# Five projections of an attention kernel moved within its four-step rhythm

## What is computed

```python
# layers 0, 1, 2, each with its own weights (W.T in layer 2)
q = heads(x @ W_q); k = heads(ctx @ W_k); v = heads(ctx @ W_v)
x = merge(softmax(q @ k.T / sqrt(8)) @ v) @ W_out + b_out + x

# layer 3: text = ctx[:, :73], ip = ctx[:, 73:]
probs_t = softmax(q @ k_t.T / sqrt(8))
text_out = merge(probs_t @ v_t)
qsem = l2norm(probs_t @ text)                  # per head, 256 channels
sem = qsem @ l2norm(ip).T
probs_ip = softmax(q @ k_ip.T / sqrt(8) + 0.5 * sem) * spatial_mask
x = (text_out + merge(probs_ip @ v_ip)) @ W_out + b_out + x
```

## Time and profile before

| what | us |
|---|---|
| median of 3 runs | 2264.24 |
| lowest, highest | 2257.44, 3683.89 |
| the profiled execution, its own time | 2264.95 |
| its span, first to last instruction | 2263.2 |
| PE busy with matmuls, weight loads | 2086.4, 1697.5 |
| DVE busy | 1481.7 |
| ACT busy | 1075.1 |
| POOL busy | 458.7 |

### The profile page before, as it was taken

How to read it: one execution, slowest core, us unless ns; L and a number is a source line. 1 busy time by engine, 2 the same in 40 slices (tenths; PEclk the granted TensorE clock), 3 DMA queues, 4 the chain that set the end, 5 groups by cost and what they waited for, 6 DMA issues and landing times.

```text
span 2263.2 us, 75842 instructions
## 1 busy us (share of the span) xinstructions
PE 2086.4 (92%) x26394; PEld 1697.5 (75%) x26394; DVE 1481.7 (65%) x4449; ACT 1075.1 (48%) x2733; POOL 458.7 (20%) x870
## 2 busy tenths in 40 slices
PE   2699999999999999999999999999999999999975
PEld 1567877887787788778778877887887788778764
DVE  3236776777677676767767766776676677667654
ACT  0245554455445455544545554554554455555431
POOL 0112122212212221221222122122212222222110
PEclk9889999999999999999999999999999999999975
DMA  3111111211111121112111111211211121111000
GB/s 82 49 43 50 52 43 42 52 50 39 47 52 44 41 52 51 38 46 52 45 41 52 52 38 47 53 44 40 52 52 38 47 53 44 39 53 38 22 10 5
DMA packets 108576, 101.31 MB, mean 45 GB/s; under 512 B 42240, under 2 KB 84952, under 8 KB 108184
## 3 DMA queue, kind: packets, MB, share of 16 engines
q1 hardware_dynamic: 104556, 92.88, 15.1%
q10 hardware_dynamic: 3628, 3.33, 0.6%
HBM read 34.13 MB, written 5.41 MB: 17 GB/s over the span
## 4 chain that ended last, share of the span: by engine, by line
PE 78%; SPq 8%; DVE 5%; issue 4%; DMA 2%; ACT 2%; ACTq 1%; DVEq 0%; POOLq 0%; POOL 0%
PE ps_s L738 11%; PE ps_c L816 10%; PE ps_s L771 8%; PE ps_c L886 6%; PE ps_k L839 6%; PE ps_k L644 5%; PE ps_q L717 5%; PE ps_c L875 4%; PE ps_k L670 4%; PE ps_s L788 4%; PE ps_k L844 4%; SPq L584 3%; PE ps_c L891 3%; PE ps_c L852 2%; SPq L577 2%
## 5 line engine op out<-in xcount | busy, mean ns | idle before, releaser
L1131 DVE TENSOR_REDUCE top<-ps_s 128x6 f32<-128x462 f32 (+3 forms) x1024 | 511.3, 546 | 88.2 <-PE ps_s L738 84.3
L1027 ACT ACTIVATE p_t<-ps_s 116x512 f32<-116x512 f32 (+1 forms) x768 | 372.9, 545 | 48.9 <-PE ps_s L771 46.9
L738 PE MATMUL ps_s<-k_blocks,q_sb 32*128 32x231 f32 (+1 forms) x3584 | 347.8, 384 | 20.3 <-issue 18.5
L816 PE MATMUL ps_c<-p_t,v_rows 116*27 116x128 f32 (+1 forms) x7168 | 288.7, 284 | 14.8 <-DMA v_rows<-v_img 12.3
L738 PEld LDWEIGHTS ps_s<-k_blocks,q_sb 32*128 32x128 f32 x3584 | 229.9, 185 | 84.9 <-issue 31.3
L816 PEld LDWEIGHTS ps_c<-p_t,v_rows 116*27 116x27 f32 (+1 forms) x7168 | 214.1, 108 | 86.5 <-issue 49.3
L1055 ACT ACTIVATE o_t<-ps_c 128x256 f32<-128x256 f32 x256 | 98.1, 383 | 368.3 <-PE ps_c L875 302.7
L1354 POOL TENSOR_TENSOR k_blocks<-k_sb,mask_k 128x231 f32<-128x231 f32 x384 | 211.8, 573 | 267.6 <-PE ps_s L771 252.5
L771 PE MATMUL ps_s<-q_sb,k_blocks 32*116 32x128 f32 (+1 forms) x5376 | 223.8, 283 | 27.7 <-DMA q_sb<-top_t 15.0
L839 PE MATMUL ps_k<-gram,p_t 116*128 116x154 f32 x896 | 210.6, 317 | 41.6 <-DVE weighted L1171 41.6
L771 PEld LDWEIGHTS ps_s<-q_sb,k_blocks 32*116 32x116 f32 (+1 forms) x5376 | 186.3, 175 | 63.7 <-issue 52.0
(11 more groups left out here) (118 smaller groups left out, 3595.3 us busy)
## 6 DMA issues: line engine op xcount, KB each, us to landing
v_rows<-v_img SPq DMA_DIRECT2D x128, 227.4 KB
context<-in_ctx SPq DMA_DIRECT2D x64, 336.0 KB, 3.0
q_sb<-top_t SPq DMA_DIRECT2D x576, 6.0 KB
v_rows<-v_img SPq DMA_DIRECT2D x64, 115.2 KB
v_rows<-v_img SPq DMA_DIRECT2D x64, 112.2 KB
v_rep<-v_dram SPq DMA_DIRECT2D x64, 50.0 KB
q_sb<-top_t SPq DMA_DIRECT2D x192, 2.0 KB
gram<-g_img SPq DMA_DIRECT2D x64, 46.3 KB
```

Of the source, the lines that this page charges most:

```text
L738: ins = pe.matmul(ps_s[:, z * 512 + j * GT:z * 512 + j * GT + n], q_sb[c % 3][lo:lo + QUAD, j * S:(j + 1) * S], k_blocks[c % 3][lo:lo + QU ...
L816: ins = pe.matmul(ps_c[t % 2][32 * (g % 4):32 * (g % 4) + UC, g // 4 * S:(g // 4 + 1) * S], v_rows[b % NC][0:n, v:v + UC], p_t[c % 3][0:n, ...
L1027: act.activation(to, source, ACT.Exp, scale=SCALE).then_inc(p_ready, 1)
L1131: dve.tensor_reduce(top[c % 2][:, z * BH:z * BH + m], s.rearrange("p (h t) -> p h t", t=T)[:, :, 0:n], AX.X, ALU.max).then_inc(s_top, 1)
```

## The change

It moves work between places of the four steps, and cuts the values in another way. No arithmetic is left out or added.

- `keys` of layers 1 and 2 go from step 2 to step 3, behind `queries` (PE); ACT copies them behind its `queries`.
- The waves go in the order z = 3, 0, 1, 2 (`BANKS`): the small one in step 1 behind `project_out`, z = 0 at that step's end, z = 1 in step 2 behind `project_out` (where the keys stood), z = 2 at its end.
- The values are made in two units, each with all three head slots of two layers: 224 and 112 columns (`values_unit`). The first stands in step 3 behind `project_out`, the second at the step's end, behind the Gram matrix, which itself moves behind `turn_back`. ACT copies each unit with three operations of 112 columns (`values_out`) instead of two of 224 and one of 224.
- ACT: in step 3 keys, products and values stand ahead of `text_exps`; the fourth of these goes to the step's end. `image_exp` of step 1 goes from between the exponents to behind `queries`.
- DVE: in step 0 steps 8 to 13 of the image branch go ahead of `results`, and 14 to 18 behind. In step 1 steps 19, 20 and the weights stand ahead of the weighing. In step 2 `results` goes ahead of `new_x`.

The core of the diff, first the step of the keys, the values and the waves:

```diff
-    if t % 8 == 2:
-        return 1, (t - 2) // 8
-    if t % 8 == 6:
-        return 2, (t - 6) // 8
+    if t % 8 == 3:
+        return 1, (t - 3) // 8
+    if t % 8 == 7:
+        return 2, (t - 7) // 8
...
+            def values_unit(b, u):
+                w = wv[:, :].rearrange("p (l k a n) -> p l k a n", l=L, k=2, a=2)[:, 2 * u:2 * u + 2]
+                third = w.rearrange("p l k a (g i d) -> p l k a g i d", g=TRI, i=2)
+                for kt in range(2):
+                    pe.matmul(ps_k[0:T, 0:2 * VN].rearrange("p (l n) -> p l n", l=2), cx(b, kt, 0, T),
+                              w[:, :, 0, kt, :], start=kt == 0, stop=kt == 1)
+                for kt in range(2):
+                    ins = pe.matmul(ps_k[0:T, 2 * VN:VU].rearrange("p (l g d) -> p l g d", l=2, g=TRI),
+                                    cx(b, kt, 0, T), third[:, :, 1, kt, :, 1, :], start=kt == 0, stop=kt == 1)
+                return ins
...
             def gram_wave(k, t, i):
-                z = 2 * (t % 4 - 1) + i
+                z = BANKS[2 * (t % 4 - 1) + i]
```

PE's function `step`:

```diff
-                if e_values(t):
-                    values(k, t)
+                if e_keys(t) and t % 4 == 3:
+                    keys(k, t)
                 if exists(t - 2):
                     product(k, t - 2)
                 if out(t):
                     project_out(k, t)
...
-                if e_gram(t):
-                    image(k, t)
-                if e_waves(t) and t % 4 == 1:
+                if e_values(t):
+                    values(k, t)
+                if e_waves(t):
                     gram_wave(k, t, 0)
-                if e_keys(t) and t % 4 == 2:
-                    keys(k, t)
...
                 if exists(t - 1):
                     second(k, t - 1)
-                if e_waves(t) and t % 4 == 2:
-                    gram_wave(k, t, 0)
                 if exists(t - 2):
                     turn_back(k, t - 2)
                 if e_waves(t):
                     gram_wave(k, t, 1)
                 if e_keys(t) and t % 4 == 0:
                     keys(k, t)
+                if e_gram(t):
+                    image(k, t)
                 if e_values(t):
                     values_rest(k, t)
```

ACT's:

```diff
+                if ip(t - 6):
+                    image_exp(k, t - 6)
+                if e_keys(t) and t % 4 == 3:
+                    keys(k, t)
+                if exists(t - 2):
+                    products(k, t - 2)
                 if e_values(t):
                     values(k, t)
...
                 if ip(t):
+                    for i in range(3):
+                        text_exps(k, t, i)
+                if exists(t - 1):
                     for i in range(4):
-                        text_exps(k, t, i)
-                for i in range(2):
-                    if exists(t - 1):
-                        exps(k, t - 1, i)
-                if ip(t - 6):
-                    image_exp(k, t - 6)
-                for i in range(2, 4):
-                    if exists(t - 1):
                         exps(k, t - 1, i)
...
                 if e_values(t):
                     values_rest(k, t)
+                if ip(t):
+                    text_exps(k, t, 3)
```

DVE's, its end:

```diff
                 if ip(t - 5):
                     norms(k, t - 5)
                     image_branch(k, t - 5, 1, 8)
...
+                if ip(t - 5):
+                    image_branch(k, t - 5, 8, 14)
                 if exists(t - 2):
                     results(k, t - 2)
...
                 if ip(t - 5):
-                    image_branch(k, t - 5, 8, 16)
+                    image_branch(k, t - 5, 14, 19)
```

More of the change, by code:

```diff
@@ L47 @@
 VL = TRI * UC
+VU = 2 * (VN + TRI * D)
 LEAD = 128
@@ L986, in values, with values_out @@
                     act.wait_ge(v_ready[(b - 1) % NC], loads(k, b - 1, NC, per=4))
-                for i in range(2):
-                    ins = act.activation(v_img[i][:, :].rearrange("p (g u) -> p g u", u=UC)[:, :, i * D:(i + 1) * D],
-                                         ps_k[0:T, 0:L * VN].rearrange("p (g u) -> p g u", u=2 * D)
-                                         [:, :, i * D:(i + 1) * D], ACT.Copy)
-                ins.then_inc(va_evac, 1)
+                values_out(0).then_inc(va_evac, 1)
+            def values_out(u):
+                for i in range(GH):
+                    to = v_img[i][:, 2 * u * VL:2 * (u + 1) * VL].rearrange("p (g u) -> p g u", u=UC)
+                    if i < 2:
+                        source = ps_k[0:T, 0:2 * VN].rearrange("p (g u) -> p g u", u=2 * D)[:, :, i * D:(i + 1) * D]
+                    else:
+                        source = ps_k[0:T, 2 * VN:VU].rearrange("p (g u) -> p g u", u=D)
+                    ins = act.activation(to[:, :, i * D:(i + 1) * D], source, ACT.Copy)
+                return ins
             def values_rest(k, t):
@@ L1293, in step @@
                             less_top(k, t, i)
-                if e_waves(t) and t % 4 == 1:
+                if ip(t - 6):
+                    image_branch(k, t - 6, 19, 21)
+                    image_weights(k, t - 6)
+                if e_waves(t):
                     weigh(k, t, 0)
```

52 lines of the change are left out of this document (15 added, 37 removed).

## The result

The changed kernel takes 2284.5 us (median of 7 runs, 2276.9 to 2285.5) against 2265.1 us for the kernel before (7 runs beside it): ratio 1.0085, 95% interval 1.0066 to 1.0103. It is 0.85% slower, which by the bound of 2% counts as no difference. One execution of the kernel before took 3683.89 us; it is left out of the ratio. The prediction was 2285. In the two profiled executions the spans are 2282.9 and 2263.2 us, so 19.7 us apart, the very sum that the prediction had. But that sum was to come from the periods alone, and only part of it does.

What follows compares the result with a forecast made beforehand. It took the chain of waits between engines, not TensorE's apparent fullness, as the bound. Per full period +0.37-0.97+0.36+0.70 = +0.46 us, over 58 periods 19.7 us on 2264.95, gave 2285 us; forecast 2272 to 2300 (chance 0.48), range 2240 to 2312.

Steps and rivals of the forecast that it cites:

- Waves apart: Step 2's `second` to the next `turn_out`: 3.70 instead of 4.67 us, a gain of 0.97; stall moves to `ps_s` banks.
- full periods: Four-step periods where all terms apply, +0.46 us each; 39 were counted with this loss.
- Keys and values in step 3: `turn_out` to `second` of step 3: keys and first unit replace the large values pass and Gram pair, a 0.36 us loss.
- Behind `second` of step 3: `second` to next `turn_out`: ACT's copies and text exponents delay the exponents, 4.59 instead of 3.89 us, a 0.70 loss.
- DVE in steps 0 and 1: Branch steps, two held by POOL, delay `results` and `top_of`; `second` of step 1 comes 0.60 us late.
- the covered periods: Two periods in six (image tokens, loop's branch): PE is late in step 0 and covers DVE; +0.09 us each, 19 counted.
- Number of periods: 58 of the 64 periods count, since PE idles in first and last: 39x0.46+19x0.09 = 19.7 us.
- SP, "cost nothing" and "a floor": SP's later `place_values` costs nothing; its DMAs for visit 1's tops set a floor for gains in steps 1 and 2.
- Rival 1: Nothing moves: DVE slips between POOL's operations, loses 0.3 instead of 0.60, copies take 0.12 less; 2265 to 2270 us; chance 0.25.
- Rival 2: Faster: ACT does not hold PE in step 3 and DVE's lag is covered, -0.69 a period, 2225 us; chance 0.14.
- Rival 3: Over 2% slower: DVE loses one more whole POOL operation in steps 8 to 13, +1.02 a period, 2324 us; chance 0.10.
- Rival 4: The eight added weight loads count at 0.07 each, +0.56 a period, 2317 us; chance 0.03.

Runs made afterwards that it cites:

- The experiment with the text exponents: Changed kernel with ACT's first three `text_exps` of step 3 ahead of its copies of the values: 2248.8 us, ratio 0.9941.
- The kernel with the values issued first: Changed kernel with `results` first, text exponents first, branch steps 14 to 18 behind `top_of`, and SP's values DMAs ahead of visit 0's tops: 2144.6 us.
- the first experiment with POOL: Changed kernel with POOL's masked keys of layer 1 written for 2 of the 77 tokens only: 2284.6 us, ratio 1.0098.
- The experiments that lift the two conditions: Changed kernel with three text exponents ahead of ACT's copies (2248.8 us), or `results` ahead of branch steps 8 to 13 (2276.7 us); both: 2238.7 us.

## Why the prediction came out right, and what it missed

**Waves apart, -0.97: right.** -0.94 in the mean and -0.97 in full periods. The stall went from DVE's weighing to the banks of the scores, as said: the wave ahead of `turn_out` of step 3 takes 1.33 in the mean where it took 0.99.

**Keys and values in step 3, +0.36: right.** +0.34 in the mean, +0.40 in a full period. Both passes were priced 0.1 low (1.23 for a unit instead of 1.14, 1.60 for the old pass instead of 1.50), and the difference of the two was not. At t=148 the kernel before waits 0.33 more ahead of `second`, behind the Gram matrix, for DVE's `less_top`. The list of waits has 12 for it before and 3 after, so that it is gone from the loop, and the loss is only 0.07 in that period. The prediction had not seen it.

**Behind `second` of step 3, +0.70: right.** +0.70, +0.81 and +0.62 in neighbouring periods, +0.61 in the mean. The experiment with the text exponents shows that it is the queue on ACT.

**DVE in steps 0 and 1, +0.60: the mechanism and the mean of a full period right, the covered periods wrong.** The two held operations are there, and the lag of 0.77 too, at t=144. (The prediction's own terms come to 1027.32 and so to 0.74, and 1030.42 with 0.3 to 1030.72, a loss of 0.54 and not 0.60.) At t=148 and 152 the lag is only 0.51 and 0.55, so that "full period" was not one kind. The loss up to `second` of step 1 is +0.75, +0.48 and +0.53 at the three and +0.56 at t=136, 0.58 in the mean of these. The prediction then supposed that PE covers DVE's lag in two periods of six. It does so in one, where the image tokens come in, and there the small wave comes through as well: -0.55. Behind the loop's branch the loss is +0.42. These two nearly cancel, so that +0.36 is measured in the mean of all, where 0.60 in 39 of 58 periods gives 0.40.

**Number of periods.** The prediction had 0.34 in the mean ((39 x 0.46 + 19 x 0.09)/58), and 0.31 is measured. By the prediction's own 58 periods that is 18 us. By kind, over the whole loop, the four sorts of full period change by +0.73, +0.10, +0.45 and +0.29, 0.39 in the mean for the 0.46 forecast, and the two others by +0.26 and -0.02, 0.12 for 0.09.

**SP, "cost nothing" and "a floor": half right.** In full periods PE hardly waits for the tops (-0.08 at all three). But `turn_image` to `second` of step 2 is +0.05 in the mean and not -0.08: in the period with the image tokens the stretch is 5.84 and was 5.19, and `turn_top` there takes up to 1.87 where 0.20 is enough. That is the floor of which the prediction spoke: it takes back the gain that the small wave has in this very period. And SP is where the one large miss lies, the start. The prediction left the first and last periods out "since PE idles" in them. The waits of PE between 60 and 215 us, of the kernel after:

```profile
PE ps_c L821 <- DMA v_rows<-v_img: 15.4, 4, 5.3
PE ps_s L776 <- DMA q_sb<-top_t: 10.7, 5, 4.6
```

The kernel before has 12.3 and 1.6 there: +12.2 of the 14.3 us. The granted clock from 50 to 100 us is 0.70 of full speed after, and 0.90 before; 28 records of `product` take 1.92 us where PE has waited, and 1.07 in full swing. The kernel with the values issued first has 0.73 from 50 to 100 us and still the shortest start, so that the clock of that stretch does not decide alone. That the transfers' place in SP's queue is behind it is shown by that kernel: its step 20 begins at 188.0 us, and at 208.3 in the one that differs from it in this alone. In the changed kernel it is 209.0, in the kernel before 194.6. The DVE part alone does not lengthen the start (193.6), the old order of the waves and the old cut do not mend it (207.9 and 209.1). ACT's order has a part in it: with the text exponents first it is 206.0. The rest should come with the values and keys in their new places; which of the two it is was not separated.

**The end, not foreseen.** Behind step 236 the changed kernel needs 11.5 us less, and all of it falls behind step 252. One row of each between 2100 and 2200 us (the columns are PE, PEld, DVE, ACT, POOL, then the granted clock): before and after

```profile
2100.00:2200.00 100.00, 81.60 (x924) 67.06 (x924) 61.77 (x189) 38.39 (x94) 15.57 (x29) 0.87 0.07 18
```

```profile
2100.00:2200.00 100.00, 92.55 (x1150) 77.85 (x1143) 69.59 (x214) 47.36 (x121) 19.12 (x38) 0.93 0.10 27
```

The runs lie at different places in the program here, by about 20 us, so that the row says no more than that PE is fuller. 4.2 us of the 11.5 are the weighing (7.3 us of waits behind 2050 before, 3.1 after), and the DVE part alone gives 12.2 there in its one profiled execution, while the changed kernel with `results` first again loses 4.8 of the 11.5 (26.4 us before from step 266 to 270, 21.2 after, 25.8 with `results` first). So the end seems to be DVE's doing. It rests on single executions: the first experiment with POOL, which changes nothing else, differs by 1.5 there. Why a lag in full periods shortens the end was not looked into.

So the sum agrees to 1 us because +14.3 and -11.5, which no step of it had, nearly cancel, and that is luck. The periods' part was forecast as 19.7 for 58 of them, 18.3 for 54, and is 16.9; that much was worked out.

**The rivals.** Rival 1 (nothing moves) fell by the held operations. Rival 2 supposed that ACT does not hold PE and that DVE's lag is covered, at 2225 us. "ACT's queue has no way around the copies" is true of the queue as it was written. The experiments that lift the two conditions reach 2248.8 (ACT) and 2276.7 (DVE), and together 2238.7. Against the kernel before that is 0.56 a period and not 0.69, by what `top_of` still costs, and the longer start stays. Rival 3 (one more whole POOL operation) was not seen: two were held, as counted. At t=148 and 152 a third, step 9, takes 0.29 beside POOL's `mark` of 0.32, so that the way it named exists, at 0.11 us and not at 0.56. Rival 4, the weight loads, fell: the old pass of 448 columns with four loads takes 1.60, and the unit of 336 columns with eight takes 1.23, where the columns alone make 1.20 of it.

## What to carry to other kernels

A stall removed from one engine's chain is not gained until the next releaser at the following wait has been named. Here that was DVE's `top_of`, behind it SP's queue, and each edit showed its worth only when the one behind it had been made (the small wave: nothing that could be measured, then 30 us). When operations are moved on an engine that works in order, look at what stands directly ahead of those that another engine waits for. Three short exponents behind three copies cost 0.77 us in a full period, four DMA issues ahead of four others 0.8. And a change in steady state should be counted in the start and the end of the program too: both moved by more than 10 us here.

## What the runs showed of the hardware that was not expected

A DMA issue for the tops or the values holds SP for 0.64 to 0.84 us (the eight in a row from 1202.53 on, above): four tops of 2 to 6 KB take 3.1 us, four of the values with 112 to 227 KB 3.2. So twelve in a row, with those of the Gram matrix, are 10 us, a third of a period. What was transferred counted less than what stood ahead of it.

A DVE operation of 0.18 us took 0.46 or 0.50 beside a POOL operation of 0.57, 0.29 beside one of 0.32, and 0.22 beside one of 0.20. In these rows the hold ended with the other's operation, and shorter POOL operations alone took 27 us off this kernel.

`second` of step 1 to the next operation of PE takes 1.24 in the mean after and 1.09 before, mostly 1.29 where PE had waited at `turn_top` just ahead. No run here separates why.
